# The memory stage turned on its side: channels on the partitions, scans on VectorE, and the dispatch stage run beside it

## Chip, cores and metric

The kernel runs on one core of a Trainium2 chip. The metric is the device time of one execution in microseconds (us): 490.81 us, the median of 3 runs (489.8 to 494.01). A core has five engines with an in-order instruction stream each: TensorE (PE), VectorE (DVE), ScalarE (ACT), GpSimd (POOL) and SyncE (SP, which here only issues DMAs). They meet through semaphores.

## What is computed

A layer with two halves on x of shape (4, 1024, 128), all in float32. The first half is a memory with decaying weights:

```
z      = x @ W_in                          # 128 key values, 32 scores, 256 query values
z_mem  = causal convolution of 4 taps over the first 160
p_w    = exp(clip(score_scale * s_raw, -20, 20) + log_tw)      # (b, l, 32)
phi    = k_val[..., None] * theta                              # (b, l, 32, 4, 8)
den    = cumsum(p_w, axis=l)
num_re = cumsum(p_w * cos(phi), axis=l);  num_im = cumsum(p_w * sin(phi), axis=l)
out_re = sum_m(num_re/den * q_re + num_im/den * q_im)          # and out_im likewise
y      = silu(out_re * coef + out_im * coef')                  # (b, l, 128)
x1     = layernorm(x + y @ W_out)
```

The second half is a mixture of experts: the router picks 2 of 8 experts for a token by x1 @ router_w.T, each expert is relu(x W)^2 W', a ninth, shared one takes every token, and out = layernorm(x1 + the weighted sum). A cumulative sum over 1024 tokens for each of 4 sequences x 1024 channels (32 x 4 x 8), twice, is the large part of the first half.

## The kernel before

There are four stages, each a function that returns one instruction stream per engine: `memory`, `dispatch`, `routed`, `finish`. The order on each engine is written out by hand; dispatch hooks its first pieces into the last tiles of memory by `tail(i)`, and does the rest in `rest()`.

**memory** goes over 32 tiles of 128 tokens (4 sequences in turn). Tokens are on the partitions and the 1024 channels lie along the free dimension. For each tile: `phases` (PE, L604) makes theta times key into a PSUM pair of banks, `rounding` (ACT, L383) and `fraction` (DVE, L748) take it to a fraction of a turn, `fold`, `sine` and `cosine` (ACT, L387, L390, L394) make both features, `weigh` (POOL, L495) multiplies them by p_w, `carry` (POOL, L503) adds the running total of the tile before by a small DMA, `sums` (PE, L620) does the cumulative sum over the 128 tokens as four matmuls with a triangular matrix, `read_out` (DVE, L769) multiplies by the query, and `reduce_most`/`reduce_halved` (DVE, L787, L795) sum over m. `last_row` (ACT, L403) keeps the total for the carry. `feat` has 4 buffers.

**dispatch** goes over 8 groups of 512 tokens: y is turned by PE and projected by W_out, then `residual` (DVE, L1238, L1241, L1244, L1246: residual sum and statistics), `normalise` (L1253 to L1260), `choose` (L1266 to L1279: the two best experts), `place` and `count` (L1290 to L1295, L1283, L1285: each token's slot), the shared expert (`up` L998, `relu` L1116, `square` L1122, `down` L1008), and `scatter` (POOL, L1192): two indirect DMAs for each 128 tokens, 64 in all, which put x1 and its weight into a table in HBM sorted by expert. The table is first filled with blanks by 68 DMAs of SP (L349). `table_of_tiles` makes the list of tiles.

**routed** takes 46 tiles from the table through their experts (L1500, L1513) and **finish** adds up and normalises. The first up-projection of routed (L1500) starts at 332.5 us of the profile, which is used below as the place where the front of the kernel ends.

Before the memory stage PE is kept busy with ten small matmuls (L626). The main loop of DVE in memory is

```
if i + 3 < NT:
    fraction(i + 3)
read_out(i, (0, 1) if i else (1,))
...
```

## Time and profile before

| | |
|---|---|
| runs | 490.81 us median, 489.8 to 494.01 |
| span of the profiled execution | 498.7 us, 7644 instructions |
| busy, share of the span | PE 91%, DVE 72%, ACT 71%, POOL 63% |
| granted TensorE clock, mean | 0.974 |
| DMA | 48.56 MB, mean 97 GB/s |
| chain that ended last, by engine | PE 40%, POOL 22%, DVE 16%, issue 8%, ACT 7% |

The span of the profiled execution is 7.9 us longer than the median of the runs. A row of a group of instructions gives line, engine, operation, output and inputs, shapes and the count, then busy time in us and the mean ns of one, then the idle time ahead of them and what released it. The busy time of a group counts overlapping instructions once. A float32 matmul stands in the trace as two records, so that x256 are 128 matmuls.

### The profile page before, as it was taken

Reading aid. Unit: us, or ns where it says so; the run is one execution under the profiler, and the core shown is the slowest. Engines: PE = TensorE matmul, PEld = TensorE weight load, DVE = VectorE, ACT = ScalarE, POOL = GpSimd, SP = SyncE. Lnnn points to the kernel's source line nnn. Section 1 sums busy time; section 2 is a strip of 40 time slices with the busy share of each in tenths; the row PEclk is TensorE's granted clock in tenths of the full one; section 3 lists DMA queues with packets and bytes.
Section 4 is the critical chain, followed back from the end, with each engine's and each line's share of the span. In section 5 each row is a group of like instructions: output and inputs, shape, how many; then the busy total and the mean of one; then the engine's idle time right before and its main releaser. Section 6 shows DMA issues by size and latency. Waiting matters only on the chain.

```text
span 498.7 us, 7644 instructions
## 1 busy us (share of the span) xinstructions
PE 453.9 (91%) x2184; PEld 293.6 (59%) x2184; DVE 356.7 (72%) x873; ACT 354.5 (71%) x557; POOL 315.1 (63%) x285
## 2 busy tenths in 40 slices
PE   8997999999999988798898898489999999999983
PEld 5332444444344333455576675389999999899721
DVE  5898999999999999998688964353333333455246
...
GB/s 274 8 122 43 86 146 213 216 196 151 130 153 131 151 133 148 3 1 33 39 45 43 45 43 47 46 94 51 72 65 81 71 60 58 60 57 67 11 324 182
DMA packets 41193, 48.56 MB, mean 97 GB/s; under 512 B 5616, under 2 KB 25266, under 8 KB 41152
## 3 DMA queue, kind: packets, MB, share of 16 engines
...
q10 hardware_dynamic: 144, 0.31, 0.2%
q14 instruction: 23, 0.19, 0.1%
...
## 4 chain that ended last, share of the span: by engine, by line
PE 40%; POOL 22%; DVE 16%; issue 8%; ACT 7%; DMA 2%; another core or an unknown queue 2%; DVEq 0%; POOLq 0%; SPq 0%; ACTq 0%
POOL memory_feat L495 17%; PE routed_ph L1500 13%; PE routed_po L1513 12%; PE dispatch_sph L998 4%; PE dispatch_spo L1008 3%; POOL memory_feat L503 2%; DVE memory_prod L769 2%; DVE memory_y_raw L778 2%; POOL memory_prod L518 2%; PE memory_nsum L620 1%; ACT finish_xo L1714 1%; PE routed_px L1488 1%; PE dispatch_plr L969 1%; DVE memory_feat L769 1%
## 5 line engine op out<-in xcount | busy, mean ns | idle before, releaser
L495 POOL TENSOR_TENSOR memory_feat<-memory_feat,memory_p_tok 128x1024 f32<-128x1024 f32 x64 | 125.9, 2063 | 17.1 <-ACT memory_feat L390 14.2
L620 PE MATMUL memory_nsum<-memory_feat,tri 128*128 128x512 f32 x256 | 118.1, 604 | 6.3 <-ACT memory_last_rows L403 2.4
L1476 POOL DMA_INDIRECT pick_scratch<-routed_ob,routed_xg x71 | 71.6, 1008 | 75.1 <-DVE routed_ob L1597 56.7
L1192 POOL DMA_INDIRECT table_scratch<-dispatch_xrow,dispatch_slot x64 | 61.9, 967 | 40.9 <-PE dispatch_sph L998 18.9
L620 PEld LDWEIGHTS memory_nsum<-memory_feat,tri 128*128 128x128 f32 x256 | 47.8, 192 | 65.1 <-issue 56.2
L1546 ACT ACTIVATE routed_rel<-routed_ph 128x512 f32<-128x512 f32 x71 | 42.3, 597 | 47.7 <-PE routed_ph L1500 46.7
L1513 PE MATMUL routed_po<-routed_w2c,routed_hid 128*128 128x128 f32 x568 | 71.3, 276 | 1.2 <-DVE routed_ob L1597 0.7
L1500 PE MATMUL routed_ph<-routed_xs,routed_w1c 128*128 128x256 f32 (+1 forms) x368 | 71.1, 337 | 1.2 <-DVE routed_w2c L1583 0.9
L1597 DVE TENSOR_SCALAR routed_ob<-routed_po,routed_xg 128x128 f32<-128x128 f32 x71 | 22.6, 347 | 69.2 <-issue 49.6
L769 DVE TENSOR_TENSOR memory_prod<-memory_nsum,memory_query 128x1024 f32<-128x1024 f32 x58 | 68.8, 1216 | 1.9 <-PE memory_nsum L620 1.8
L1513 PEld LDWEIGHTS routed_po<-routed_w2c,routed_hid 128*128 128x128 f32 x568 | 67.0, 192 | 1.9 <-issue 1.1
L1500 PEld LDWEIGHTS routed_ph<-routed_xs,routed_w1c 128*128 128x128 f32 x368 | 56.5, 191 | 6.2 <-ACT routed_xs L1537 1.8
L403 ACT COPY memory_last_rows<-memory_nsum 32x1024 f32<-32x1024 f32 x56 | 54.2, 1005 | 3.5 <-DVE memory_prod L769 2.6
L1116 ACT ACTIVATE dispatch_srel<-dispatch_sph 128x512 f32<-128x512 f32 x32 | 19.1, 596 | 38.4 <-PE dispatch_sph L998 29.8
L1008 PE MATMUL dispatch_spo<-w,dispatch_shid 128*128 128x128 f32 x256 | 36.0, 295 | 8.2 <-ACT dispatch_shid L1122 8.2
L1008 PEld LDWEIGHTS dispatch_spo<-w,dispatch_shid 128*128 128x128 f32 x256 | 34.4, 209 | 14.4 <-ACT dispatch_shid L1122 8.6
L1555 ACT ACTIVATE routed_hid<-routed_rel 128x512 f32<-128x512 f32 x71 | 42.5, 638 | 0.0
L748 DVE SCALAR_TENSOR_TENSOR memory_feat<-memory_feat,memory_ph 128x1024 f32<-128x1024 f32 x32 | 38.7, 1209 | 5.3 <-ACT memory_feat L383 4.5
L787 DVE TENSOR_REDUCE memory_y_raw<-memory_prod 128x96 f32<-128x1536 f32 x24 | 41.8, 1741 | 0.0
L604 PE MATMUL memory_ph<-setup_th_f,setup_k_val 64*128 64x512 f32 x128 | 36.8, 651 | 4.4 <-DVE memory_feat L748 4.4
L394 ACT ACTIVATE memory_feat<-memory_feat,memory_half_pi 128x1024 f32<-128x1024 f32 x32 | 36.5, 1140 | 0.0
L998 PE MATMUL dispatch_sph<-dispatch_x1T,w 128*128 128x512 f32 x64 | 35.0, 636 | 1.1 <-DVE memory_feat L769 1.1
...
## 6 DMA issues: line engine op xcount, KB each, us to landing
...
```

Of the source, the lines that this page charges most:

```text
L403: nc.scalar.copy(last_rows[32 * b:32 * b + 32, h * NF:(h + 1) * NF], nsum[96:P, h * NF:(h + 1) * NF]).then_inc(rows_kept, 1)
L495: nc.gpsimd.tensor_tensor(v, v, pv, ALU.mult).then_inc(wfeat_done, 1)
L620: last = nc.tensor.matmul(nsum[:, o:o + 512], tri[:], feat[:, i % U, h, q * 512:(q + 1) * 512], start=True, stop=True)
L769: nc.vector.tensor_tensor(products(i)[:, h, :].rearrange("p (q r c) -> p q r c", q=KQ, r=REP), nv, qv.unsqueeze(2).broadcast_to([P, KQ, RE ...
L998: nc.tensor.matmul(sph[q % 2][:], w1[:, E, q * P:(q + 1) * P], x1T[:, g % XR].rearrange("p t c -> p (t c)"), start=True, stop=True).then_i ...
L1008: last = nc.tensor.matmul(spo[g % 2][:, t * D:(t + 1) * D], shid[:, g % 2, q, t * P:(t + 1) * P], w2[:, E, q, :], start=(q == 0), stop=(q ...
L1192: nc.gpsimd.indirect_dma_start(out=table, in_=xrow[:, r, n, :], in_offset=None, out_offset=bass.IndirectOffsetOnAxis(ap=slot[:, r, n:n + 1 ...
L1476: nc.gpsimd.indirect_dma_start(out=pick_dram, in_=ob[:, u, h, :], in_offset=None, out_offset=bass.IndirectOffsetOnAxis(ap=xg[:, t % XU, h, ...
L1500: last = nc.tensor.matmul(ph[s][:, q * n:(q + 1) * n], w1c[:, u, q * P:(q + 1) * P], xs[:, s, 0:n], start=True, stop=True)
L1513: last = nc.tensor.matmul(po[:, h * D:(h + 1) * D], hid[:, s, q * n + h * P:q * n + (h + 1) * P], w2c[:, u, q, :], start=(q == 0), stop=(q ...
L1546: nc.scalar.activation(rel[:, n % 2, :], ph[s][:, o:o + FC * P], ACT.Relu).then_inc(rel_done, 1)
L1555: nc.scalar.activation(hid[:, s, o:o + FC * P], rel[:, n % 2, :], ACT.Square).then_inc(hid_done, 1)
```

## The change

`memory` and `dispatch` become one function `front`, with channels on the partitions and tokens along the free dimension. Its loop has 43 steps `s`; the first 32 are units: 128 channels (q, h, m for one of the 8 repeats) x 1024 tokens of one sequence.

- The cumulative sum is a `tensor_tensor_scan` on DVE over 1024 tokens, one for each of the two features: state = state * abc + feature. `abc` is the ratio of the weights of neighbouring tokens, which PE spreads from 32 rows to 128 partitions into a pair of PSUM banks (`broadcast`); so the multiplication by p_w, the triangular matmuls, the last rows and the carry DMAs go away. A factor `c` (weight over denominator) is multiplied in at the end.
- POOL multiplies the scanned feature by the query (`product`); PE sums over m with a matrix of zeros and ones (`gathered`, eight matmuls of 32 columns out); DVE scales two units at a time (`scaled`, 128 x 256); ACT does SiLU; SP carries the block to its channel partitions by four DMAs of SBUF to SBUF (`move`), which stand ahead of that step's blank fills.
- One PSUM bank (`kq`) serves keys, queries and factors, one piece a step (`feed`).
- The eight dispatch groups start at steps `BASE` = 10, 14, 18, 22, 26, 30, 34, 35 and go one stage a step: project, measure, normalise, choose, place; scatter over four steps; the shared expert beside it, with one PSUM bank for both projections, and x and x1 added by PE.
- The warming matmuls are gone. `feat` has 5 buffers. `routed` and `finish` stay as they are but for the address of the output rows. The loads are the same weights, in another order.

The diff, cut to what is spoken of below:

```diff
-            for i in range(NT):
-                weigh(i)
-                if i >= B:
-                    carry(i)
-                if i - 2 in HALVED:
-                    halve(i - 2)
-                tail(i)
+BASE = (10, 14, 18, 22, 26, 30, 34, 35)
+LAST = BASE[-1] + 8
+PROLOGUE_Q = 4
...
+        def kq_work(s):
+            b, n = s // REP, s % REP
+            if b == B - 1:
+                return ("c", b, n) if n < 2 else None
+            if n < 2:
+                return ("v", b + 1, n)
+            if n < 4:
+                return ("c", b, n - 2)
+            return ("q", b + 1, n - 4)
...
+            def move(n):
+                b, g = n // PAIRS, n % PAIRS
+                s.wait_ge(silu_done, n + 1)
+                if b >= 2:
+                    s.wait_ge(proj_done, 2 * (b - 1))
+                for q in range(QT):
+                    s.dma_start(yT[2 * QH * g:2 * QH * (g + 1), b % 2, q * QL:(q + 1) * QL],
+                                  y_pair[2 * QH * q:2 * QH * (q + 1), n % 2]).then_inc(y_moved[n % 2], 16)
...
+            for i in range(1, NU + 3):
+                s.wait_ge(scan_done, 2 * min(i, NU))
+                if 3 <= i <= NU + 1 and i % 2:
+                    move((i - 3) // 2)
...
+        def scalar(act):
...
+            rounding(0)
+            for b in range(1, B):
+                exps(b)
+            nc.scalar.activation(warm[:], half_pi[:], ACT.Silu)
+            keep_query(0, 0)
+            features(0)
+            keep_query(0, 1)
+            rounding(1)
+            keep_query(0, 2)
+            features(1)
+            keep_query(0, 3)
+            rounding(2)
+            for s in range(LAST):
+                for g in range(NG):
+                    if stage(g, s) == 7:
+                        keep_shared(g)
+                if s + 2 < NU:
+                    features(s + 2)
+                for g in range(NG):
+                    if stage(g, s) == 2:
+                        keep_x(g)
+                if s + 3 < NU:
+                    rounding(s + 3)
+                if s < NU:
+                    keep(s)
+                if 3 <= s <= NU + 1 and s % 2:
+                    silu((s - 3) // 2)
...
+                    elif k == 3:
+                        weigh(g)
+                        hidden(g, 0)
+                        hidden(g, 1)
+                    elif k == 4:
+                        hidden(g, 2)
+                        hidden(g, 3)
...
+        def gpsimd(pool):
...
+            for s in range(LAST):
+                for g in range(NG):
+                    k = stage(g, s)
+                    if k == 1:
+                        inverse_root(g)
+                    elif 4 <= k < 8:
+                        scatter(g, k - 4)
+                if s < NU:
+                    product(s, 0)
+                    product(s, 1)
...
         def tensor(pe):
...
+            def broadcast(i):
+                b, n = i // REP, i % REP
+                if n == 0:
+                    pe.wait_ge(rr_ready, min(b, 1) + 1)
+                if i:
+                    pe.wait_ge(scan_done, 2 * i)
+                def quarter(q):
+                    return nc.tensor.matmul(abc[:, q * QL:(q + 1) * QL],
+                                            spread[q * K:(q + 1) * K, n].rearrange("p c m -> p (c m)"),
+                                            rr[q * K:(q + 1) * K, b, 1:], start=True, stop=True)
+                quarter(0)
+                quarter(2).then_inc(abc_even, 1)
+                pe.wait_ge(abc_even, i + 1)
+                quarter(1)
+                quarter(3).then_inc(abc_done, 1)
...
+            for b in range(1, B):
+                scores(b)
+            phases(0)
+            pe.wait_ge(wq_made, 1)
+            pe.wait_ge(lw_ready, B)
+            for n in range(PROLOGUE_Q):
+                if n:
+                    pe.wait_ge(kq_kept, n)
+                ask(0, n).then_inc(kq_done, 1)
+                if n < 2:
+                    phases(n + 1)
+            for s in range(LAST):
+                if s < NU:
+                    broadcast(s)
+                if s + 3 < NU:
+                    phases(s + 3)
+                for g in range(NG):
+                    k = stage(g, s)
+                    if k == 0:
+                        project(g)
+                    elif k == 2:
+                        turn_x(g)
+                    elif k == 3:
+                        up(g, 0)
+                    elif k == 4:
+                        up(g, 2)
...
+                if 0 < s <= NU:
+                    gathered(s - 1)
+                if s < NU:
+                    feed(s)
+                for g in range(NG):
+                    k = stage(g, s)
+                    if k == 2:
+                        route(g)
+                    elif k == 3:
+                        up(g, 1)
+                        rank(g)
+                    elif k == 4:
+                        up(g, 3)
+                    elif k == 5:
+                        down(g, (0, 1))
+                    elif k == 6:
+                        down(g, (2, 3))
...
+        def vector(dve):
...
+            def cumulated(i):
+                dve.wait_ge(abc_done, i + 1)
+                for h in range(2):
+                    dve.wait_ge(feat_done, 2 * i + 1 + h)
+                    v = feat[:, i % U, h]
+                    nc.vector.tensor_tensor_scan(v, abc[:], v, 0.0, ALU.mult, ALU.add).then_inc(scan_done, 1)
...
+            for s in range(LAST):
+                if s + 2 < NU:
+                    fraction(s + 2)
+                for g in range(NG):
+                    k = stage(g, s)
+                    if k == 4:
+                        place(g)
+                        count(g)
+                    elif k == 1:
+                        measure(g)
+                    elif k == 2:
+                        normalise(g)
+                    elif k == 3:
+                        choose(g)
...
+                if 3 <= s <= NU + 1 and s % 2:
+                    scaled((s - 3) // 2)
+                if s == 0:
+                    quarter_sums()
...
+                if s < NU:
+                    cumulated(s)
```

Not shown: `denominators` (a scan and a clamp over 128 x 256) and `invert` (a reciprocal and a product over 128 x 256) for each of the 4 sequences, and `ratios` (three operations over 128 x 771 for three sequences at once), all on DVE; `offsets`, one small matmul.

## Rows read from the trace of the kernel before

**Rows 1.** Busy time by stretch: us, then each engine's busy time (instructions), PE clock, DMA.

```profile
64.00:196.00 132.00, 129.14 (x351) 53.61 (x350) 129.06 (x126) 130.78 (x140) 118.59 (x91) 1.00 0.48 167
226.00:332.50 106.50, 88.24 (x512) 65.73 (x511) 73.17 (x361) 51.67 (x108) 61.87 (x64) 0.94 0.15 46
332.50:471.00 138.50, 136.87 (x1007) 128.64 (x1008) 57.60 (x162) 90.40 (x188) 70.60 (x70) 1.00 0.22 62
```

**Rows 2.** Chain that ended last, in order of time: start, us, what.

```profile
179.73 4.04 POOL memory_feat L495 x2
...
332.55 3.69 PE routed_ph L1500 x16
```

**Rows 3.** Timeline of the start: start, us, engine, line, instruction, idle before it.

```profile
5.80 1.13 PE L553 MATMUL memory_pq<-memory_xT,memory_wconv 128*128 128x128 f32 x8 [0.19 <-DMA memory_xT<-x_T]
...
22.18 1.22 DVE L769 TENSOR_TENSOR memory_prod<-memory_nsum,memory_query 128x1024 f32<-128x1024 f32 x1
...
38.34 1.28 ACT L447 ACT_TABLE_LOAD   x1
...
42.19 1.76 PE L604 MATMUL memory_ph<-setup_th_f,setup_k_val 64*128 64x512 f32 x4 [3.42 <-DVE memory_feat L748]
```

**Rows 4.** Groups by line and form: the scans of the kernel before.

```profile
L728 DVE TENSOR_TENSOR_SCAN setup_den<-setup_one_row,setup_den,setup_pT 128x512 f32<-128x512 f32 x1 | 1.3, 1284 | 0.1
...
L728 DVE TENSOR_TENSOR_SCAN setup_den<-setup_one_row,setup_pT 128x512 f32<-128x512 f32 x1 | 1.2, 1214 | 0.0
...
L1308 DVE TENSOR_TENSOR_SCAN dispatch_whole<-dispatch_one,dispatch_whole 128x8 f32<-128x8 f32 x1 | 0.2, 204 | 0.0
```

**Rows 5.** Groups by line and form: operations that the change keeps, or near ones.

```profile
L495 POOL TENSOR_TENSOR memory_feat<-memory_feat,memory_p_tok 128x1024 f32<-128x1024 f32 x64 | 125.9, 2063 | 17.1 <-ACT memory_feat L390 14.2 <-ACT memory_p_tok L363 2.7
...
L748 DVE SCALAR_TENSOR_TENSOR memory_feat<-memory_feat,memory_ph 128x1024 f32<-128x1024 f32 x32 | 38.7, 1209 | 5.3 <-ACT memory_feat L383 4.5
...
L387 ACT ACTIVATE memory_feat<-memory_feat 128x1024 f32<-128x1024 f32 x32 | 33.7, 1054 | 1.7 <-DVE memory_feat L748 1.7
...
L1116 ACT ACTIVATE dispatch_srel<-dispatch_sph 128x512 f32<-128x512 f32 x32 | 19.1, 596 | 38.4 <-PE dispatch_sph L998 29.8 <-remote 5.8 <-issue 2.6
...
L739 DVE RECIPROCAL memory_inv_den<-memory_inv_den 128x128 f32<-128x128 f32 x8 | 7.5, 941 | 0.0
```

**Rows 6.** Groups by line and form: matmuls on the whole array and on half of it.

```profile
L620 PE MATMUL memory_nsum<-memory_feat,tri 128*128 128x512 f32 x256 | 118.1, 604 | 6.3 <-ACT memory_last_rows L403 2.4 <-DVE memory_feat L769 2.0 <-DMA memory_feat<-memory_last_rows 1.4
...
L604 PE MATMUL memory_ph<-setup_th_f,setup_k_val 64*128 64x512 f32 x128 | 36.8, 651 | 4.4 <-DVE memory_feat L748 4.4
...
L1008 PE MATMUL dispatch_spo<-w,dispatch_shid 128*128 128x128 f32 x256 | 36.0, 295 | 8.2 <-ACT dispatch_shid L1122 8.2
```

**Rows 7.** Timeline of DVE in dispatch: choose; place, count and root; normalise; measure.

```profile
221.49 0.18 DVE L1266 COPY dispatch_lg<-dispatch_plr 128x32 f32<-128x32 f32 x1
...
223.13 0.19 DVE L1279 TENSOR_TENSOR dispatch_sel<-dispatch_hot 128x32 fp32r<-128x32 f32 x1
...
225.51 0.18 DVE L1290 TENSOR_TENSOR dispatch_base<-dispatch_plr,dispatch_off 128x32 f32<-128x32 f32 x1
...
227.22 1.12 DVE L1260 TENSOR_SCALAR dispatch_xrow<-dispatch_res,dispatch_mv,dispatch_root 128x128 f32<-128x128 f32 x4
...
229.17 0.87 DVE L1241 BATCH_NORM_STATS2 dispatch_stats<-dispatch_res 128x6 f32<-128x128 f32 x4
...
230.49 0.17 DVE L1246 TENSOR_SCALAR dispatch_var<-dispatch_mv 128x4 f32<-128x4 f32 x1
```

**Rows 8.** Timeline of POOL at the end of dispatch: scatters one behind another, and the last.

```profile
318.98 0.96 POOL L1192 DMA_INDIRECT table_scratch<-dispatch_xrow,dispatch_slot  x1 [0.30 <-issue]
320.25 0.95 POOL L1192 DMA_INDIRECT table_scratch<-dispatch_xrow,dispatch_slot  x1 [0.30 <-issue]
...
324.55 0.95 POOL L1192 DMA_INDIRECT table_scratch<-dispatch_xrow,dispatch_slot  x1 [0.34 <-ACT dispatch_shid L1122]
```

**Rows 9.** DMA issues: KB each, median us from issue to landing.

```profile
memory_feat<-memory_last_rows POOLq DMA_DIRECT2D x28, 8.0 KB, 2.1
```

1692 lines of the change are left out of this document (655 added, 1037 removed).

## The prediction, made before the changed kernel ran

> **What bounds the kernel now.** I read the busy time by stretch first. From 64 to 196 us the memory stage has PE, DVE and ACT busy 98 to 99% of the time and POOL 90% [rows 1]: four engines are balanced, and the chain of waits goes through POOL's `weigh` there, in pieces like 4.04 us for two, from 64 to 196 us [rows 2]. So no single engine's saving shortens this stage. From 226 to 332.5 us (dispatch) DVE is busy 73.2 of 106.5 us, PE 88.2 and POOL 61.9: here there is idle time to win by putting dispatch beside memory. From 332.5 to 471 us PE is busy 136.9 of 138.5 us; routed and finish are not changed, so I carry their 166.2 us (332.5 to 498.7) over whole. The question is when the first up-projection of routed starts, 332.55 us now [rows 2].
>
> **Price of a scan.** 512 columns took 1.21 and 1.28 us, 8 columns 0.20 us [rows 4]: 2.0 to 2.1 ns a column, while an ordinary two-input operation of 1024 columns takes 1.21 us in all [rows 5]. A scan of 1024 is then 2.27 to 2.37 us; its state hangs on the column before, so I see no reason for less. Two of them, the second overlapping the first's tail by 0.1 us: 4.5 us a unit, 144 us for 32. This is the largest new term, all on DVE. It replaces two products and the reductions on DVE, `sums` on PE (118.1 us), and the last rows and carries on ACT and POOL.
>
> **DVE's work from the first scan to the last** (start to start, so operations of 1.21 count 1.14):
> - scans, 32 x 4.5 = 144
> - `fraction`, 29 left after the first three, x 1.14 = 33
> - `scaled`, 15 of 128 x 256: between 0.17 for 4 columns [rows 7] and 1.21 for 1024 [rows 5], 0.43 each, 6
> - denominators and inverse, 4 times: scan of 256 0.73, clamp 0.3, reciprocal 2 x 0.94 [rows 5], product 0.43, together 3.3: 13
> - ratios, 3 operations of 771 columns at 0.95, and constants 0.5: 3
> - dispatch: measure 1.4 (229.17 to 230.6), choose 1.76, place and count 1.12, root steps and normalise 1.7, token copy and chain waits 0.4: 6.4 a group [rows 7]; five groups and one measure before the last scan, 33.
>
> Sum 232, say 233 us. Steps 0 to 10 cost 6.2 us of DVE, later ones 7.8. Before, DVE was busy 129.1 + 73.2 = 202 us in the two stretches of [rows 1], which leave out the first 64 us and the 30 between them. So the change does not lighten DVE: it packs its work more closely, and adds a start and a tail.
>
> **When the first scan starts.** Before, the first full-width read-out ran at 22.18 us, and the first matmul on x at 5.80 [rows 3]. Now PE does from 5.8: keys of the first sequence, 8 matmuls of 512 at 118.1/128 = 0.92 [rows 6], 7.4; scores, 64 matmuls of 32 columns out, four side by side, some 0.5 for four, 8; `phases(0)` 1.1; 22.3. The warming matmuls are gone: a pair of phases took 1.76 us after PE had been idle 3.42 us [rows 3], against 36.8/32 = 1.15 on average [rows 6]; the start loses some 2 us to this: 24.5. From there the order is a ping-pong written into ACT, PE and DVE: rounding 1.0, six exponentials 2.1, a table load 1.28 [rows 3] with its warm-up 0.2, a query 0.5, features 3.0 (three of 1.05 [rows 5]), query 0.5, rounding 0.9: 34. Then `fraction(1)` 1.1, `phases(2)` 1.2, a query matmul 0.9, its copy 0.6, features 3.0, query 0.5, rounding 0.9, `fraction(2)` 1.2 and `quarter_sums` 1.1, ahead of the first scan in DVE's order: 45 us. If half of the ping-pong overlaps, 38; with slow clock at each gap, 48. So the scans start about 20 us later than the read-outs did.
>
> **What PE adds.** A step's PE work: `broadcast` two pairs of K=32, 256 columns, with a wait between, 1.3; `phases` 1.0; `gathered` 1.0; `feed` 3.6 for keys (steps 0, 1 of 8), else 0.9; dispatch in four steps 1.85 + 1.8, 2.7 (down: 128 columns, 36.0/128 = 0.28 us each, back to back some 0.9 for four [rows 6]), 0.5 + 0.9 + 1.8, 2.65. Heavy steps reach 9.5 to 11 us against DVE's 7.8. A late PE delays `broadcast`, and so the scans; DVE's work ahead of them hides about 1.6 us. `up(g, 1)` and `up(g, 3)` stand behind `feed` and wait for a ReLU (0.60 [rows 5]) that stands behind ACT's `keep`; `turn_x` waits for `normalise`; all hold what is queued behind them on PE, `rank` and the next `broadcast`. By steps of eight this comes to 9 us once (steps 16 to 23), 3 before and 4 behind. `project` of groups 0, 2, 4 needs y blocks that SP carries: a POOL DMA of 8 KB landed in 2.1 us [rows 9], four issues and the landing make 3.5 us behind SiLU, and PE stands 2 to 3 us in `project`, 1 of which comes through. Low bound: all hidden but the one value pair, 5. High bound 28. I take 18, nearest to the count. Last scan ends at 45 + 233 + 18 = 296 us.
>
> The row on half-array matmuls bears on this. A pair of phases on the two halves of the array takes 1.15 us [rows 6] where one full matmul of the same columns takes 0.92, so 0.2 us are lost around the pair. The Trainium skill (TensorEngine Tiling (Array Packing), Key Properties) says that changing the tiling mode drains the engine; the new step has four such changes (K=32, full, 32 columns out, full), which by that rule and that row is 0.8 us of a step, and without them PE would be nearly hidden.
>
> **The tail.** From the last scan's end T: last product 2.0 [rows 5], gathered 1.0, behind it the chain of group 5 (turn, route, choose) to T+6.7, scaled and SiLU T+7.6, four DMAs T+11.3, project 6 T+13.2, measure, root, normalise 6 T+17.6, turn, route T+20, choose T+22, `rank(6)` behind `turn_x(7)` on PE T+26, `place(6)`, choose 7, `rank(7)` behind `up(7, 1)` T+33, slots T+34. Scatters come every 1.27 us [rows 8]; two of group 6's pairs are out by then, six pairs remain: 15 us, T+49. Before, from the start of the last scatter (324.55) plus 0.95 to the first up-projection were 7 us [rows 8, 2]: T+56. If ranks don't wait for `up`, T+50.
>
> So routed starts at 296 + 56 = 352 us, 19.5 behind 332.5. ACT's group of ReLUs shows one stall of 5.8 us put down to nothing on the core [rows 5] (all engines stood); 332.5 holds it, my 352 does not. I add 3 for such. Profile: 498.7 + 22.5 = 521.2 us. The profiled execution is 7.9 above the median of the runs, so 513 us.
>
> **The rivals.**
> - *DVE packs without a wait and the start overlaps* (the faster side, one mechanism: cross-engine waits vanish in the slack of the 5 feature buffers). It decides from below 18 us of start and wait savings: start at 30 (bound by x and PE alone), PE waits 5, tail 55: 30 + 233 + 5 + 55 = 323, 9.5 below, 481 us. For it: buffers of 5 and phases three units ahead. Against it: `fraction(2)` stands ahead of the first scan, and the queries' single bank is waited for each time. Chance 0.08.
> - *Waits small, start as I say*: 40 + 233 + 8 + 51 = 332, no change: 491 us. Chance 0.12.
> - *PE becomes the bound*, by the clock: PE has 4.8 us of work in steps 0 to 10 and waits for each scan's end; PE at 2 to 3 us of idle showed the slow clock [rows 3], and 4.8 doubled is over DVE's 6.2. At 1.5 us more for 11 steps, and heavy steps unhidden: +20 on mine, 533 us. Chance 0.2.
> - *POOL becomes the bound*: products 2 x 2.06 at most [rows 5], two scatters 2.53 and a quarter of a root 0.3 are 6.9 us a step against 7.8. It doesn't, unless DVE slows POOL; within the next rival's price. That the change does not do what it says is not open: the scans must run.
>
> **How the numbers follow.** Forecast (DVE-bound with PE's waits, late start) 0.6, at 513; its own range, from the bounds of start (38 to 48), waits (5 to 28) and tail (50 to 60), 498 to 530. The range over cases leaves out the fastest rival and half of "no change" below and the far end of the clock case above: 494 to 534. One per cent is about what a measurement can tell from no change. Faster by over 1%: 0.08; within: 0.11; slower: 0.81.
>
> **What would show it.** In the changed profile: the scan group at 2.2 to 2.4 us mean, x64; first scan at 45 us; the last scan ending at 285 to 305; DVE busy 85 to 93% between; idle PE ahead of broadcasts in the first ten steps, late broadcasts as DVE's wait in steps with keys; last scatter some 50 us behind the last scan; routed as long as before (138.5 us). I am wrong if a scan takes near 1.2 us, if the first starts by 30, or if the last scatter stands within 35 us of the last scan.

## The result, and the profile after

The changed kernel takes 569.58 us (median of 5 runs, 566.18 to 570.44) where the kernel before takes 490.81: a ratio of 1.157, 95% interval 1.153 to 1.162. The direction was forecast, the size was not: 513 us was said, with 534 as the upper end. Some executions of three kernels below (one of four of e5 and of e9, two of four of e17) ran 1 to 2% longer at a lower granted clock; the times given leave them out.

The profiled execution has a span of 564.4 us. By stretches (columns as in [rows 1]: the busy times are those of PE, its weight loads, DVE, ACT and POOL): units 0 to 9, units 10 to 31 in two rows, the tail up to the first up-projection of routed, and routed with finish:

```profile
46.30:126.00 79.70, 65.55 (x318) 25.06 (x314) 72.03 (x55) 47.73 (x59) 46.65 (x20) 0.79 0.29 96
126.00:200.00 74.00, 61.79 (x338) 30.70 (x339) 62.83 (x104) 43.85 (x63) 47.53 (x26) 0.86 0.24 82
200.00:324.50 124.50, 106.75 (x650) 57.55 (x649) 112.55 (x183) 76.87 (x111) 93.73 (x59) 0.89 0.29 97
324.50:397.90 73.40, 50.22 (x234) 34.00 (x235) 30.60 (x146) 22.00 (x45) 32.49 (x32) 0.78 0.23 75
397.90:564.40 166.50, 156.20 (x1051) 137.69 (x1049) 69.46 (x240) 103.71 (x228) 76.31 (x75) 0.97 0.31 91
```

Between the first scan (46.3 us) and the end of the last (324.5) DVE is busy 247.4 of 278.2 us and PE 234.1. No engine is full, as three were in the memory stage before [rows 1], and PE is granted a mean clock of 0.79 to 0.89 where it had 1.00. Routed and finish take 166.5 us, as before. The chain that ended last now runs through PE for the most part, and POOL is nearly gone from it:

```profile
PE 56%; DVE 24%; ACT 6%; issue 5%; DMA 3%; POOL 2%; SPq 1%; DVEq 0%; ACTq 0%; POOLq 0%
```

DVE's groups between first and last scan (line, operation, count, busy us, mean ns, idle before and its releaser):

```profile
L897 DVE TENSOR_TENSOR_SCAN front_feat<-front_abc,front_feat 128x1024 f32<-128x1024 f32 x64 | 142.9, 2275 | 15.2 <-PE front_abc L684 15.0
...
L932 DVE TENSOR_TENSOR front_newton<-front_var,front_root 128x4 f32<-128x4 f32 x6 | 12.2, 2028 | 0.0
...
L880 DVE TENSOR_TENSOR_SCAN front_cc<-front_pw,front_offs 128x256 f32<-128x256 f32 x4 | 5.5, 1383 | 0.0
...
L926 DVE TENSOR_SCALAR front_var<-front_mv 128x4 f32<-128x4 f32 x6 | 4.9, 816 | 0.2
L974 DVE TENSOR_TENSOR front_hit<-front_base,front_hot 128x64 f32<-128x64 f32 x5 | 3.4, 680 | 0.2
```

The scan costs what [rows 4] said, 2.275 us for 1024 columns. But an operation on 4 columns (L932) takes 2.03 us, and a scan of 256 columns 1.38 us where 0.73 was reckoned. Those lines are the first surprise; the second is the clock, the third the tail.

### The profile page after: what moved, and what is told of

Its sections match the earlier page's. It is cut to its first block, busy times and chain, and to the rows that moved or that the text cites. A ratio compares the mean times of both kernels' runs of the same rounds, so it can differ in the third digit from the quotient of the medians.

```text
span 564.4 us, 8480 instructions
## 1 busy us (share of the span) xinstructions
PE 471.1 (83%) x2760; PEld 296.8 (53%) x2760; DVE 366.5 (65%) x772; ACT 312.6 (55%) x531; POOL 302.5 (54%) x223
## 4 chain that ended last, share of the span: by engine, by line
PE 56%; DVE 24%; ACT 6%; issue 5%; DMA 3%; POOL 2%; SPq 1%; DVEq 0%; ACTq 0%; POOLq 0%
DVE front_feat L897 12%; PE routed_ph L1205 12%; PE routed_po L1218 11%; PE front_abc L684 4%; PE front_d L770 4%; PE front_yb L700 4%; PE front_kq L630 3%; DVE front_feat L890 2%; PE front_d L781 2%; PE front_ph L672 2%; POOL table_scratch L603 2%; PE front_kq L636 2%; DVE front_newton L932 2%; PE front_abc L630 2%; DVE front_xrow L939 2%
## 5 line engine op out<-in xcount | busy, mean ns | idle before, releaser
L590 POOL TENSOR_TENSOR front_feat<-front_feat,front_query 128x1024 f32<-128x1024 f32 x64 | 149.2, 2352 | 106.6 <-DVE front_feat L897 106.3
L897 DVE TENSOR_TENSOR_SCAN front_feat<-front_abc,front_feat 128x1024 f32<-128x1024 f32 x64 | 142.9, 2275 | 15.2 <-PE front_abc L684 15.0
L603 POOL DMA_INDIRECT table_scratch<-front_xrow,front_slot x64 | 62.8, 982 | 50.7 <-DVE front_slot L977 34.3
L684 PE MATMUL front_abc<-front_rr,front_spread 32*128 32x256 f32 x256 | 51.4, 481 | 17.5 <-DVE front_feat L897 15.2
L890 DVE SCALAR_TENSOR_TENSOR front_feat<-front_feat,front_ph 128x1024 f32<-128x1024 f32 x32 | 38.3, 1198 | 16.9 <-ACT front_feat L456 16.9
L672 PE MATMUL front_ph<-front_k_val,front_th 32*128 32x512 f32 x128 | 42.0, 737 | 6.4 <-DVE front_feat L890 6.4
L684 PEld LDWEIGHTS front_abc<-front_rr,front_spread 32*128 32x128 f32 x256 | 21.6, 205 | 47.7 <-DVE front_feat L897 21.3
L461 ACT ACTIVATE front_feat<-front_feat 128x1024 f32<-128x1024 f32 x32 | 33.7, 1052 | 23.2 <-DVE front_feat L890 23.2
L700 PE MATMUL front_yb<-front_feat,front_gather 128*32 128x256 f32 x512 | 42.4, 458 | 2.7 <-DVE front_y_pair L905 2.7
L770 PE MATMUL front_d<-front_x1T,front_w1s 128*128 128x512 f32 x48 | 31.9, 751 | 14.6 <-ACT front_srel L494 14.6
L464 ACT ACTIVATE front_feat<-front_feat,front_half_pi 128x1024 f32<-128x1024 f32 x32 | 36.3, 1134 | 0.0
L456 ACT ACTIVATE front_feat<-front_ph 128x1024 f32<-128x1024 f32 x32 | 32.4, 1013 | 6.3 <-PE front_ph L672 6.1
L462 ACT ACTIVATE front_feat<-front_feat 128x1024 f32<-128x1024 f32 x32 | 33.3, 1042 | 0.0
L700 PEld LDWEIGHTS front_yb<-front_feat,front_gather 128*32 128x32 f32 x512 | 15.0, 124 | 31.5 <-issue 18.8
```

The costliest lines, as they stand in the source:

```text
L590: nc.gpsimd.tensor_tensor(v, v, query[:, b % 2, h], ALU.mult).then_inc(prod_done, 1)
L603: nc.gpsimd.indirect_dma_start(out=table, in_=xrow[:, k, g % XG, t, :], in_offset=None, out_offset=bass.IndirectOffsetOnAxis(ap=slot[:, k, ...
L672: last = nc.tensor.matmul(ph[:, h * HL:(h + 1) * HL], th[q:q + 2 * QH, n].rearrange("p c m -> p (c m)"), k_val[q:q + 2 * QH, b % 2, h * HL ...
L684: return nc.tensor.matmul(abc[:, q * QL:(q + 1) * QL], spread[q * K:(q + 1) * K, n].rearrange("p c m -> p (c m)"), rr[q * K:(q + 1) * K, b ...
L700: last = nc.tensor.matmul(yb[2 * QH * q:2 * QH * (q + 1), 0:QL], gather[:, n], feat[:, i % U, h, q * QL:(q + 1) * QL], start=(n == 0 and h ...
L770: nc.tensor.matmul(mlp_bank[g], w1s[:, q * P:(q + 1) * P], x1T[:, g % 2].rearrange("p t c -> p (t c)"), start=True, stop=True).then_inc(up ...
```

## The experiments

All times are medians; each kernel was timed beside the kernel before on the same chip, which stood at 491.45 to 492.14 us each time. e3, e5, e6, e9 and e16 leave out part of what the layer computes. "Unit n at" is when the first scan of unit n starts, the tail is from the end of the last scan to the first up-projection of routed, both in the profiled execution. Edits are against the changed kernel if nothing else is said. The table is put together from the profiles:

```
kernel                       us     unit 0  unit 10  last scan ends  tail
changed                     569.6    46.3    124.3       324.5       73.4
changed, once more  (e8)    567.2    45.8    123.4       326.7       73.4
e1  fill, start and 1-9     566.4    46.5    123.5       327.9       73.4
e2  rank first              560.3    46.9    123.1       325.4       68.3
e3  product of 4 columns    551.4    47.1    120.0       314.3       70.0
e4  one unit early          568.8    34.9    123.9       327.7       73.1
e5  thin shared expert      570.5    46.2    121.1       332.3       72.1
e6  half scans              550.3    47.2    115.4       307.3       73.7
e7  y moves last            570.2    47.2    123.5       329.8       72.9
e9  half scans, fill        558.1    44.9    111.0       314.2       75.4
e10 broadcast ahead         638.7    46.8    140.9       398.4       73.4
e11 two units early         563.8    35.7    118.7       322.3       73.1
e12 e2, e10, e11 together   624.5    33.1    129.8       381.9       70.4
e13 gathered late           588.0    46.8    133.7       354.2       70.8
e14 e2, fill in the tail    562.0    46.0    123.7       325.6       68.2
e15 e2, e11, e13 together   575.1    35.6    128.0       342.1       65.5
e16 half scans, e13         569.1    46.2    129.5       328.1       74.8
e17 e13, fill               598.8    47.3    125.0       359.3       71.6
e18 e15, fill               572.7    33.5    115.1       337.2       64.5
```

**The changed kernel once more.** It tells the noise between chips and executions: 2.4 us in the median, 2 us in the last scan's end.

> The changed kernel itself, beside the other three on the same chip, so that their differences are read against it: 566 to 571 us. If its time is below 563 us, the gain read from the kernel with rank first is partly one of the chip.

It ran at 567.2 us (564.6 to 571.7).

**GpSimd's product holds up VectorE.**

```diff
-                nc.gpsimd.tensor_tensor(v, v, query[:, b % 2, h], ALU.mult).then_inc(prod_done, 1)
+                nc.gpsimd.tensor_tensor(v[:, 0:4], v[:, 0:4], query[:, b % 2, h, 0:4], ALU.mult).then_inc(prod_done, 1)
```

> The changed kernel with GpSimd's product of feature and query on 4 columns instead of 1024 (this leaves the query out of nearly all of the read-out). Theory A (GpSimd's two-input product holds up VectorE's two-input operations): VectorE's busy time between the first and the last scan falls from 247 to 233 to 236 us, newton steps take 0.2 instead of 2.0 us, the last scan ends at 306 to 312 us, the time falls by 15 to 20 us. Theory B (the operations of VectorE are long for themselves, the stretch is set by TensorE's clock and waits): VectorE's busy time stays above 243 us and the time falls by at most 4 us, by the shorter tail.

551.4 us, 16 to 18 less. DVE's busy time between the scans fell from 247.4 to 226.4 us, more than expected. The same groups in this kernel, in the same stretch:

```profile
L897 DVE TENSOR_TENSOR_SCAN front_feat<-front_abc,front_feat 128x1024 f32<-128x1024 f32 x64 | 143.0, 2276 | 23.2 <-PE front_abc L684 23.1
...
L932 DVE TENSOR_TENSOR front_newton<-front_var,front_root 128x4 f32<-128x4 f32 x6 | 0.9, 153 | 0.0
...
L880 DVE TENSOR_TENSOR_SCAN front_cc<-front_pw,front_offs 128x256 f32<-128x256 f32 x4 | 3.0, 747 | 0.0
...
L926 DVE TENSOR_SCALAR front_var<-front_mv 128x4 f32<-128x4 f32 x6 | 1.3, 224 | 0.2
...
L974 DVE TENSOR_TENSOR front_hit<-front_base,front_hot 128x64 f32<-128x64 f32 x5 | 1.1, 227 | 0.2
```

L932 is 0.15 us instead of 2.03, the scan of 256 columns 0.75 instead of 1.38, an operation with one tensor operand (L926) 0.22 instead of 0.82. The large scan, which reads its ratios from PSUM, is the same in both. The timeline of the changed kernel shows what a small operation waits for:

```profile
138.47 4.67 POOL L590 TENSOR_TENSOR front_feat<-front_feat,front_query 128x1024 f32<-128x1024 f32 x2 [4.36 <-DVE front_feat L897]
...
141.60 1.56 DVE L932 TENSOR_TENSOR front_newton<-front_var,front_root 128x4 f32<-128x4 f32 x1
...
323.22 4.63 POOL L590 TENSOR_TENSOR front_feat<-front_feat,front_query 128x1024 f32<-128x1024 f32 x2
```

L932 ends at 143.16 us, 0.02 behind the product's end at 143.14. So operations of DVE with two operands in SBUF that start under a running product of 2.35 us stand behind it, some with one operand too, and those with a PSUM operand do not: theory A. The Trainium skill (SBUF — State Buffer, SBUF: two separate sides) calls the port pair that POOL and DVE share an exclusive lock, held for a whole instruction by an operation of POOL, against which a DVE operation with two SBUF inputs or in a 2-port mode waits. The trace agrees for the end of the wait, but one operation can wait for more than one product: in the tail L932 starts at 324.39 us under the first of the last two products, takes 3.48 us and ends at 327.87, with the second (327.85).

But only 11 of the 21 us came through to the last scan; DVE waited for `broadcast` 23.1 us instead of 15.0. The short product also frees `gathered` sooner on PE, and the run does not tell the two effects apart in the time.

**Less work for VectorE.** Each scan over half of the tokens.

```diff
-                    nc.vector.tensor_tensor_scan(v, abc[:], v, 0.0, ALU.mult, ALU.add).then_inc(scan_done, 1)
+                    nc.vector.tensor_tensor_scan(v[:, 0:HL], abc[:, 0:HL], v[:, 0:HL], 0.0, ALU.mult, ALU.add
+                                                 ).then_inc(scan_done, 1)
```

> The changed kernel with each scan over 512 of the 1024 tokens (this leaves half of the cumulated sums out, and takes 64 times 1.14 us, 73 us, from VectorE). Theory A (VectorE's load sets the pace, at 89% busy): the last scan ends 45 to 60 us sooner, at 265 to 280 us. Theory B (TensorE at 84% busy and its order set the pace together with VectorE): the last scan ends only 15 to 30 us sooner, TensorE's idle time between the scans falls below 10%.

DVE's busy time between the scans fell from 245.7 (the changed kernel once more) to 189.2 us, the last scan came 19 us sooner. (The scans themselves fell by 68 us, 142.9 to 74.6, but some small operations are held longer: the one of L926, L927 in this kernel, takes 1.59 us instead of 0.82.) Theory B, then: DVE alone does not set the stretch. These are the rows of the half scans, from first scan to last and from unit 10 to the last (columns as above):

```profile
47.20:307.30 260.10, 228.64 (x1289) 108.69 (x1286) 189.23 (x340) 167.82 (x231) 185.91 (x104) 0.87 0.29 99
...
115.40:307.30 191.90, 165.39 (x973) 84.65 (x972) 138.12 (x286) 122.12 (x175) 139.20 (x84) 0.89 0.28 94
```

DVE idles 71 of 260 us, PE 31, which is 12% and not the under 10% of theory B. Unit 10 came 8 to 9 us sooner than in the changed kernel; from there to the last scan's end it took 191.9 us, the changed kernel 200.2 and 203.3.

**Less work for TensorE.** Three of four up matmuls and all down matmuls of the shared expert on 4 columns.

```diff
-                nc.tensor.matmul(mlp_bank[g], w1s[:, q * P:(q + 1) * P], x1T[:, g % 2].rearrange("p t c -> p (t c)"),
+                w = GT * P if q == 0 else 4
+                nc.tensor.matmul(mlp_bank[g][:, 0:w], w1s[:, q * P:(q + 1) * P],
+                                 x1T[:, g % 2].rearrange("p t c -> p (t c)")[:, 0:w],
...
-                        last = nc.tensor.matmul(bank[:, t * D:(t + 1) * D], shid[:, g % 2, q, t * P:(t + 1) * P],
-                                                w2[:, E, q, :], start=False, stop=(t == GT - 1 and q == FC - 1))
+                        last = nc.tensor.matmul(bank[:, t * D:t * D + 4], shid[:, g % 2, q, t * P:(t + 1) * P],
+                                                w2[:, E, q, 0:4], start=False, stop=(t == GT - 1 and q == FC - 1))
```

> The changed kernel with the shared expert's matmuls thinned: three of four up matmuls and the 16 down matmuls of each group on 4 columns (this leaves out most of the shared expert, and takes some 6 us of TensorE's time from each of the eight groups). Theory A (from step 10 on TensorE's order is late and holds up the scans): steps 10 to 31 take 8.3 us instead of 9.3 each, last scan at 300 to 308 us, tail 5 us shorter, time 20 to 28 us less, about 544. Theory B (VectorE's own work sets the steps): the last scan ends within 6 us of 324.5, the tail is 3 to 5 us shorter, the time falls by less than 11 us.

570.5 us: no gain, where theory A had 20 to 28 us and theory B a tail 3 to 5 us shorter. From 200 us to the end of the last scan, first the changed kernel once more, then the thin one:

```profile
200.00:326.70 126.70, 110.92 (x646) 59.27 (x645) 110.82 (x183) 76.67 (x110) 93.79 (x59) 0.85 0.28 95
```

```profile
200.00:332.30 132.30, 120.60 (x642) 66.64 (x642) 108.02 (x183) 77.84 (x113) 93.77 (x59) 0.70 0.27 91
```

With fewer columns to do, PE was busy longer, 120.6 instead of 110.9 us, at a granted clock of 0.70 instead of 0.85. Less was taken out than meant: a matmul record of `down` takes 264 ns with 4 columns and 292 with 128, and the shared expert's matmuls in this stretch fell from 34.1 to 25.7 us. All other matmuls rose from 76.8 to 94.9 us. What was taken out came back as clock, and more. So this run can't tell how much the shared expert's work costs.

**Filling TensorE's idle time in the start.**

```diff
+            fill(5, cols=256)
...
                 ask(0, n).then_inc(kq_done, 1)
+                fill(2)
                 if n < 2:
                     phases(n + 1)
+                    fill(2)
...
+                if 0 < s < BASE[0]:
+                    fill(1)
```

> The changed kernel with matmuls that nobody reads on TensorE: five of 256 columns before x arrives (as the kernel before had), two of 512 behind each of the first queries and phases, and one of 512 at the end of steps 1 to 9. Theory A (the clock: TensorE waits for the scans and is granted the low level, and its chain then delays the scans): the granted clock from 46 to 126 us rises from 0.79 to 0.95 or more, the first scan comes 3 to 5 us sooner, the last scan ends at 305 to 312 us instead of 324.5, the time falls by 12 to 20 us, from 569.6 to about 553. Theory B (VectorE and the waits written into the order set the pace whatever the clock): the last scan ends within 3 us of 324.5, the time stays within 4 us of 569.6.

The clock came up (1.00 instead of 0.84 before the first scan, 0.89 instead of 0.79 from there to 126 us), and unit 10 started at 123.5 us: nothing gained, theory B for these steps, in which DVE is busy 72.0 of 79.7 us in the changed kernel. Of the start it tells less: the third query took 1.02 us instead of 2.08, but began at 38.19 instead of 36.92, behind a fill, so the fills took back there what the clock gave.

**Half scans and fill.** The fills of the start as before, and an unread matmul of 512 columns ahead of each step's `feed`, to see whether the clock is what holds the half scans.

> The kernel with half scans (each over 512 of 1024 tokens, which leaves half of the cumulated sums out) and matmuls on TensorE that nobody reads: five at the start, two of 512 columns behind each query and phases of the prologue, one of 512 columns ahead of each step's piece of feed, in all 31 steps. With half scans alone VectorE had 73 us less to do and the last scan still ended at 308 us, TensorE busy at a granted clock of 0.79 to 0.94. Theory A (what holds it there is TensorE's clock): the added work of 31 x 0.92 us raises the clock to 0.95 or more, unit 10 starts at 105 to 118 us instead of 127, the last scan ends at 280 to 300. Theory B (it is the order and the chains of waits): the clock changes nothing, the added 28 us of work make the last scan end at 308 or later.

```profile
44.90:126.00 81.10, 72.69 (x410) 30.72 (x410) 61.75 (x71) 55.30 (x68) 57.13 (x25) 0.98 0.35 115
...
111.00:314.20 203.20, 183.26 (x1016) 92.63 (x1015) 126.68 (x286) 122.50 (x175) 139.35 (x84) 0.90 0.26 89
```

Unit 10 came at 111.0 us, within theory A's 105 to 118, but the 127 us that theory A compares it with is unit 11 of the half scans; their unit 10 is at 115.4. The gain is only 4.4 us, of which 2.3 are there at the first scan. From unit 10 on the added matmuls brought no clock (0.90, and 0.89 without) and cost 11 us, and the last scan came 7 us later than with half scans alone, as theory B said. So up to unit 10 the higher clock is worth some 2 us net of the added work; behind it this run does not test the clock, since it did not rise.

**Orders: rank ahead of up.**

```diff
-                        up(g, 1)
                         rank(g)
+                        up(g, 1)
```

> The changed kernel with rank(g) ahead of up(g, 1) in TensorE's order. In the tail rank(6) stood 1.1 us and rank(7) 2.9 us behind an up at the low clock, each with a ReLU of the shared expert ahead of it. Theory A (the tail is a chain through rank): the last scatter comes 5 to 7 us sooner after the last scan (61 instead of 66.9 us), the time falls by 5 to 8 us to about 563. Theory B (the 12 last scatters on GpSimd are late anyway through the normalise and choose of group 7): less than 2 us.

560.3 us, 7 to 9 us less than the changed kernel's two medians; the tail went from 73.4 to 68.3 us. Theory A. (The rest of the difference is within what two runs of one kernel differ by.) In the changed kernel PE does this in the tail (start, us, engine, line, operation, idle before it):

```profile
361.46 2.07 PE L770 MATMUL front_ph<-front_x1T,front_w1s 128*128 128x512 f32 x2 [1.59 <-ACT front_srel L494]
...
364.04 0.37 PE L754 MATMUL front_ph<-front_seen,front_ones_r 128*128 128x32 f32 x1
...
364.45 0.19 DVE L972 TENSOR_TENSOR front_base<-front_ph,front_off 128x32 f32<-128x32 f32 x1 [5.60 <-PE front_ph L754]
...
372.73 2.05 PE L770 MATMUL front_abc<-front_x1T,front_w1s 128*128 128x512 f32 x2 [2.26 <-ACT front_srel L494]
...
375.70 0.19 DVE L972 TENSOR_TENSOR front_base<-front_abc,front_off 128x32 f32<-128x32 f32 x1 [7.71 <-PE front_abc L754]
```

The slots of a group (from L972 on) wait for `rank` (L754), which stands behind an up-projection (L770) that nobody is in need of and that itself waits for a ReLU.

**Orders: the first scans early.** First one unit, `broadcast(0)` ahead of the queries, `features(1)` ahead of the third query, and `cumulated(0)` ahead of `fraction(2)` and `quarter_sums`:

> The changed kernel with the first scans moved forward: TensorE spreads the ratios of unit 0 ahead of the queries, VectorE scans unit 0 ahead of fraction(2) and of the quarter sums, ScalarE makes the features of unit 1 ahead of the third query. Theory A (the late start moves everything): the first scan starts at 34 to 37 us instead of 46.3, the time falls by 8 to 11 us. Theory B (steps 0 to 16 are set by TensorE at the low clock, which gives the head start back): the first scan is early but the time falls by at most 3 us.

568.8 us, as theory B had it. The first scan started at 34.9 us, 11.4 sooner, and unit 1 at 54.7, only 1.7 sooner:

```profile
47.23 5.99 PE L630 MATMUL front_kq<-arena,front_wconv 128*128 128x512 f32 x8
53.15 1.25 PE L684 MATMUL front_abc<-front_rr,front_spread 32*128 32x256 f32 x6
```

The ratios of unit 1 (L684) stand behind the keys of the next sequence, 6 us at the low clock where 3.7 are needed at the high. So the second unit had to be moved too (with it, not shown here, ScalarE's features and roundings of units 1 and 2, and the offsets):

```diff
             for n in range(PROLOGUE_Q):
+                if n == 3:
+                    broadcast(1)
...
+            cumulated(0)
+            fraction(2)
+            cumulated(1)
             for s in range(LAST):
-                if s + 2 < NU:
+                if 0 < s < NU - 2:
                     fraction(s + 2)
```

> The changed kernel with the first two units scanned early: broadcast(0) ahead of the queries and broadcast(1) ahead of the last one, on VectorE scan, fraction(2), scan, then the quarter sums; the offsets behind the first piece of keys on TensorE. With only the first scan early the second one still waited until 54.7 us behind six us of keys at the low clock. Theory A (the start is a matter of order): scans of unit 1 start at 41 to 44 us, of unit 2 at 50 to 56 instead of 66.2, the time falls by 8 to 12 us. Theory B (TensorE at the low clock takes it back by step 10): unit 10 starts within 3 us of 123.4, no gain.

Unit 1 at 42.8 us, but unit 2 at 60.8, past the expected 50 to 56, and unit 10 at 118.7: 563.8 us, 3 to 6 less. Between the theories: about half of the head start is lost before unit 10.

**Orders: broadcast ahead of feed.** DVE's largest wait was for `broadcast` (15.0 us), so it was put ahead of the piece that delays it.

```diff
-                if s < NU:
-                    broadcast(s)
...
+                if s + 1 < NU:
+                    broadcast(s + 1)
                 if s < NU:
                     feed(s)
```

> The changed kernel with the ratios of unit s+1 spread (broadcast) ahead of feed(s) and of the second half of dispatch on TensorE, instead of behind them. Theory A (TensorE's order: work of the step before stands ahead of broadcast, for which VectorE waited 15 us in 10 places): the last scan ends 8 to 12 us sooner. Theory B (TensorE's throughput at its granted clock sets the stretch; what is put behind comes late elsewhere): within 4 us of 567 to 570, and TensorE waits for the scans more than 30 us instead of 15.

638.7 us, 70 more, which no theory had. DVE's wait for `broadcast` is gone (0.1 us from 126 to 300), and this came in its place:

```profile
184.47 1.90 PE L684 MATMUL front_abc<-front_rr,front_spread 32*128 32x256 f32 x8 [2.89 <-DVE front_feat L898]
...
186.30 2.07 PE L636 MATMUL front_kq<-arena,front_wq 128*128 128x512 f32 x2
...
188.41 0.58 ACT L425 COPY front_query<-front_kq 128x512 f32<-128x512 f32 x1 [9.23 <-PE front_kq L636]
...
190.28 2.07 PE L770 MATMUL front_d<-front_x1T,front_w1s 128*128 128x512 f32 x2 [1.90 <-ACT front_srel L494]
...
192.85 0.37 PE L754 MATMUL front_d<-front_seen,front_ones_r 128*128 128x32 f32 x1
...
193.27 0.19 DVE L973 TENSOR_TENSOR front_base<-front_d,front_off 128x32 f32<-128x32 f32 x1 [7.74 <-PE front_d L754]
...
194.40 2.28 DVE L898 TENSOR_TENSOR_SCAN front_feat<-front_abc,front_feat 128x1024 f32<-128x1024 f32 x1
```

PE now waits for the scan's end with the query of its step still to do; ACT copies the query before it may make features and ReLUs and waited 9.2 us; the up-projection waits for the ReLU, `rank` for the up-projection, and DVE for `rank` before it may scan. One scan to the next is a ring through PE, ACT, PE and DVE, all in series, 14.5 us for this unit. Some 17 of the 70 us arise before unit 10, where dispatch is not yet there. I read the order of the changed kernel as a compromise between two rings, not as an oversight.

> The changed kernel with all orders changed at once: the first two units early, broadcast(s+1) ahead of feed(s), rank ahead of up(g, 1), and five matmuls of 256 columns on TensorE before x arrives. If order is what cost the time (theory A), the parts add: 8 to 12 from the start, 8 to 12 from broadcast, 5 to 9 from rank, to 540 to 548 us. If clock and the hold-up of VectorE by GpSimd set it (theory B), only rank and little more stay: 556 to 562 us.

All orders together, this one with them, and five matmuls before x arrives: 624.5 us, far from both theories. The ring keeps most of its cost.

**Orders: gathered one step later.** In the changed kernel `gathered(s - 1)` waits for POOL's product and holds `feed`.

```diff
                 if s < NU:
                     broadcast(s)
+                if 1 < s <= NU:
+                    gathered(s - 2)
+                if s == NU:
+                    gathered(s - 1)
...
-                if 0 < s <= NU:
-                    gathered(s - 1)
```

`scaled` goes behind the scan of its step.

> The changed kernel with the read-out's matmuls (gathered) of a unit one step later on TensorE, right behind the next broadcast, so that feed, the keys' copy on ScalarE and the next broadcast no longer wait behind GpSimd's product of the unit before; scaled stands behind the scan of its step. Theory A (a ring through five engines sets the stretch: scan, product, gathered, feed, broadcast, scan): the last scan ends 10 to 20 us sooner, at 307 to 317 us, and TensorE waits less for GpSimd. Theory B (the stretch is the sum of VectorE's 247 us, held up by GpSimd, and dispatch's own waits): within 4 us of 325 to 327 us.

588.0 us, 18 to 21 more: neither theory. Units 4 to 8 come every 8.3 us, where the changed kernel's lightest steps take 6.0. PE never waits there, and is granted the low clock all the time (the row of 8 us, then PE in one step):

```profile
91.00:99.00 8.00, 7.93 (x30) 2.41 (x22) 5.84 (x4) 4.22 (x6) 4.66 (x2) 0.50 0.14 53
99.00:107.00 8.00, 7.93 (x32) 2.61 (x30) 5.69 (x3) 4.53 (x6) 4.65 (x2) 0.50 0.65 212
```

```profile
90.72 1.94 PE L700 MATMUL front_yb<-front_feat,front_gather 128*32 128x256 f32 x16
92.58 2.08 PE L672 MATMUL front_ph<-front_k_val,front_th 32*128 32x512 f32 x4
94.59 2.08 PE L636 MATMUL front_kq<-arena,front_wq 128*128 128x512 f32 x2
96.59 2.51 PE L684 MATMUL front_abc<-front_rr,front_spread 32*128 32x256 f32 x8
```

1.94 + 2.08 + 2.08 + 2.51 is 8.6 us, 8.3 with the overlap at their ends: here PE is the bound, and by its clock alone. That accounts for the 9 to 10 us that unit 10 is late; the other 17 to 20 us of the last scan's delay arise behind it, where PE idles 32 of 220.5 us, and no run explains them. Three of the four use 32 rows or 32 columns of the array. The sharpest test is then to give this kernel more to do:

```diff
+                if 0 < s < NU:
+                    pe.wait_ge(kq_kept, PROLOGUE_Q + min(s, (B - 1) * 8 + 2))
+                    fill(1, kq, w1s[:])
                 if s < NU:
                     feed(s)
```

> The kernel with gathered one step later, which took 588 us and in steps 3 to 8 ran at 8.3 us a step with TensorE busy all the time at the low clock (0.58), and in addition one full-width matmul of 512 columns that nobody reads ahead of each step's feed. Theory A (the low clock, which the half-array matmuls of these steps do not bring up, is what makes TensorE the bound): more work makes it faster; the clock from 46 to 126 us rises above 0.9, steps 3 to 8 take 6.0 to 6.8 us, unit 10 starts at 118 to 125 us instead of 133.7, the last scan ends 15 to 35 us sooner than 354, the time is 555 to 573. Theory B (order and waits alone): the 31 added matmuls of 0.92 to 1.84 us make it 600 us or more.

```profile
91.00:97.00 6.00, 3.76 (x18) 1.42 (x20) 5.87 (x6) 3.01 (x5) 3.70 (x2) 1.00 0.51 179
97.00:103.00 6.00, 5.33 (x36) 1.95 (x35) 5.56 (x3) 4.82 (x6) 4.63 (x3) 1.00 0.54 164
103.00:109.00 6.00, 5.25 (x32) 1.92 (x32) 5.92 (x4) 4.58 (x7) 4.64 (x3) 1.00 0.33 126
```

```profile
95.46 1.47 PE L685 MATMUL front_abc<-front_rr,front_spread 32*128 32x256 f32 x8 [2.18 <-DVE front_feat L911]
96.86 1.07 PE L701 MATMUL front_yb<-front_feat,front_gather 128*32 128x256 f32 x16
97.86 1.13 PE L673 MATMUL front_ph<-front_k_val,front_th 32*128 32x512 f32 x4
98.92 1.13 PE L790 MATMUL front_kq<-front_w1s 128*128 128x512 f32 x2
99.88 1.02 PE L637 MATMUL front_kq<-arena,front_wq 128*128 128x512 f32 x2
```

With one more whole-array matmul a step (L790) the clock is 1.00, each piece takes about half, units 5 to 7 come every 6.0 us instead of 8.3, and DVE is the bound again. Up to unit 10 theory A holds: unit 10 at 125.0 instead of 133.7. In the whole it fails: from unit 10 on, where dispatch fills PE's steps, the fill costs 14 us (220.5 us from unit 10's start to the last scan's end without it, 234.3 with it, at a clock of 0.81 and 0.83), and the time is 598.8 us, next to the 600 or more of theory B and far from the 573 of theory A.

The same pair with three orders changed:

> The changed kernel with three of the orders changed together: the first two units scanned early (5 us alone), rank ahead of up(g, 1) (7 to 9 us alone), gathered one step later. If the parts are independent: 569 less 13 less what gathering late gives alone, 538 to 556 us; if one eats the other (TensorE at the low clock between), 558 to 565.

> The kernel with three orders changed (first two units early, rank ahead of up(g, 1), gathered one step later), which took 575 us at a clock of 0.62 to 0.82, with the same added matmul a step and five at the start. Theory A (clock): 535 to 555 us, the best of all kernels with the turned memory stage, the granted clock above 0.9 from 36 to 126 us. Theory B: 590 us or more.

575.1 and 572.7 us, outside the ranges of both expectations. From unit 2 to unit 10 the one takes 67.1 us at a clock of 0.59, the other 56.4 at 0.94; behind that the fill gives most of it back (214.1 us to the last scan's end without it, 222.1 with it). The parts do add, but `gathered` late costs what the others give: 588.0 less 575.1 is 13 us for rank and the two units, which gave 7 to 9 and 3 to 6 alone.

> The kernel with half scans (half of the cumulated sums left out) and gathered one step later. Half scans alone took 73 us from VectorE and brought the last scan only 18 us forward, to 308. Theory A (the ring through product and gathered is the floor there): the last scan ends at 275 to 295 us. Theory B (another floor, TensorE's busy time at its granted clock or ScalarE's order of features and roundings): 303 to 310 us.

With half scans `gathered` late costs as much, 18.8 us (550.3 to 569.1), and the last scan ends at 328.1 us, later than either theory had it. 14 of its 21 us of delay arise before unit 10, where PE is busy 79.1 of 83.3 us at a clock of 0.64 (half scans alone: 63.3 of 68.2 at 0.81). DVE's load is not what makes `gathered` late cost.

**The tail's clock.** Two unread matmuls of 512 columns each ahead of `turn_x` and `rank` of the last two groups, beside rank first.

> The kernel with rank ahead of up(g, 1), and for the last two groups two matmuls of 512 columns that nobody reads ahead of the turn of x and ahead of rank, where TensorE stood waiting 3 to 8 us. Theory A (the tail is long by TensorE's low clock, 0.78): the granted clock in the tail rises above 0.9 and the tail from the last scan's end to the first up-projection falls from 68.3 to 62 to 65 us. Theory B (the tail is a chain of short VectorE and GpSimd operations, waits and DMAs): the clock rises but the tail stays within 2 us of 68.3.

The clock in the tail rose from 0.78 to 0.86, short of 0.9, and the tail stayed at 68.2 us (68.3 without). Theory B: a chain of short operations and waits, as far as a clock of 0.86 can show it. The thin shared expert points the same way: at a clock of 0.57 in the tail it was 72.1 us, though it had less to do there.

**The place of the y blocks in SyncE's queue.** The four DMAs of `move` behind the blank fills and weight loads of their step.

> The changed kernel with the four DMAs of a y block behind the blank fills and the weight loads of their step instead of ahead of them. Theory A (place in the queue is hidden by the steps between SiLU and project): within 2 us of the changed kernel. Theory B (project waits for the blocks, and the fills collide): 4 us or more slower, with TensorE waiting for y in project of groups 0, 2 and 4, and in the tail.

570.2 us, 0.6 to 3 more than the changed kernel's medians, with the last scan's end and the tail as there: theory A. The place in the queue is worth nothing that these runs can tell from noise.

## Why the prediction was wrong

The direction and the outline of the mechanism were right: DVE gets the scans and is not lightened, the start is later, a tail stands behind the last scan, and PE's waits come through. What failed is the price of DVE's small operations, the price of its waits, the tail, and the step from the profiled span to the median. The sum was 56.3 us short. By its terms (forecast, measured, difference):

```
first scan starts                      45      46.3     +1.3
DVE busy, first to last scan          233     247.4    +14.4
DVE idle there                         18      30.8    +12.8
tail to the first up-projection        56      73.4    +17.4
added for a stall of all engines        3       0       -3.0
routed and finish                     166.2   166.5     +0.3
from profiled span to median           -7.9    +5.2    +13.1
```

- **Price of a scan**: right (2.275 us, forecast 2.27 to 2.37).
- **The start**: right within 1.3 us, and so is the 2 us for the missing warming matmuls (the kernel before has five, ten records in its trace): the two kernels with an early start that have them again scan at 33.1 and 33.5 us, those without at 35.6 and 35.7 (34.9 with one unit early).
- **DVE's work** failed in one term. The durations came from rows in which the small operations ran alone: [rows 7] shows dispatch before, beside which POOL scattered rows and multiplied nothing. In the new kernel dispatch runs under two products of 2.35 us a unit ([rows 5] gave the product at 2.06), and the operations with SBUF operands stand behind them. The kernel with the short product has DVE busy for 226.4 us: the count of operations was even 7 us too high, and the hold-up is 21. I had looked at this the wrong way round, as a way for DVE to slow POOL, and written it off under the rival of POOL.
- **PE's waits** were taken at 18 of a range of 5 to 28; 30.8 were measured. 15.0 are the late `broadcast`, as described. The rest are waits that I had priced low or not at all: for `rank` 4.4, for `route` 4.3, for the factor c 2.4, for `project` 1.6 where 1 was said. Each stands ahead of the scan in DVE's own order. The half scans and the two orders show that this is not a margin but a second bound: taking 56 us from DVE's busy time gave 19, and putting one piece of PE in another place cost 70. The changes of tiling shape, put at four and 0.8 us a step, were not measured by themselves; `phases` runs on 32 rows too (L672 above), so that a step without dispatch has three.
- **The clock** was a rival of its own (533 us, 0.2), with 1.5 us for each of the first 11 steps. The low clock came as described, 0.79 from 46 to 126 us, but in the changed kernel it was covered by DVE (the fill gave nothing). Up to unit 10 it decides only when PE has no idle time left, as with `gathered` late (8.3 us a step). The row behind this rival had an idle time of 3.42 us ahead of it [rows 3], not 2 to 3. What the clock of 0.86 to 0.89 costs from unit 10 on, no run tells.
- **The tail**: two steps failed, with T at 324.5 us. The first is the chain of group 5, forecast as if operations took what they take alone at the high clock. The profile shows this instead:

```profile
324.39 3.48 DVE L932 TENSOR_TENSOR front_newton<-front_var,front_root 128x4 f32<-128x4 f32 x1
...
329.81 1.11 PE L733 MATMUL front_d<-ident,front_xrow 128*128 128x128 f32 x4 [5.75 <-DVE front_xrow L941]
...
332.72 3.24 PE L781 MATMUL front_d<-w,front_shid 128*128 128x128 f32 x16
...
335.79 0.40 PE L739 MATMUL front_d<-front_routerT,front_x1T 128*128 128x8 f32 x3
```

  The root step of group 5 stands 3.5 us behind the last two products; `down(4)` is 3.2 us long at the low clock and stands ahead of `route(5)`, which starts at T+11.3 where choose should have been over at T+6.7. `project(6)` comes at T+19.6 instead of T+11.3. The second is the chain of the last two groups: their slots begin at T+40.0 and T+51.2 (L972 in the rows above), where `rank` was put at T+26 and T+33. Behind that the forecast held, 22.2 us to the first up-projection where 23 were said. Of the 17.4 us at most 3.4 are the product, shown by its run; the other 14 are read from the timeline and not shown by a run. The order of `rank` and `up` is not among them: I had priced it at 6 us (T+56 against T+50), and its run gave 5.1.
- **From profile to median**: I took off 7.9 us because the profiled execution was that much above the median. But its excess lay in the stages that the change replaces (the stall of 5.8 us in [rows 5] among it), while the stretch that I carried over, 166.2 us, was as long in the new kernel. And the new kernel's profiled span was 5.2 us below its own median: 1.8 of these lie between the span (564.4) and the time (566.18) of one execution, and the profiled one was the fastest of five. 13 of the 56 us are this step and no mechanism.

The range was too narrow in its bounds as well, and its lower end does not follow from them: the lower bounds of start, waits and tail add up to 38 + 233 + 5 + 50 + 3 + 166.2 - 7.9 = 487 us, not 498. With the hold-up and the last step put right (1.8 us between span and time) and waits and tail at their upper ends of 28 and 60, the sum is 45 + 247.4 + 28 + 60 + 3 + 166.2 + 1.8 = 551 us, and 569.6 were measured: the upper ends, too, were reckoned from operations that run alone.

What stays open: how the waits in units 10 to 31 divide between clock and order. The unread matmuls hardly raised the clock there (from 0.89 to 0.90, 0.81 to 0.83 and 0.80 to 0.86) and took time themselves; a kernel with the high clock at no cost was not found. Of the kernels with the turned memory stage that compute the whole layer the one with rank first is the fastest, 560.3 us, 14% above the kernel before. No run came near the kernel before; the two units early and rank first, without `gathered` late, were not run together.
